# A fused attention and expert layer on one core: feature inputs turned by VectorE, low parts on GpSimd, gate logits behind the last expert, new orders and banks

## What is computed

```python
x = x + tanh(g_xattn) * performer(layernorm(x), ctx, ctx, random_features)
x = x + tanh(g_ffn) * ffn(layernorm(x), ...)
# performer, 16 heads of 16: q' = exp(q @ F) + eps, k' = exp(k @ F - |k|^2/2 - stab) + eps   (64 features)
#   out[t] = q'[t] . sum_{s<=t} k'[s] v[s] / q'[t] . sum_{s<=t} k'[s]
#   stab is one maximum over the keys of all batches
# ffn: h = rmsnorm(x); q = h Wq; k, v = (h Wdown) Wup; softmax over heads, per token; x += (out Wo)
#   h2 = rmsnorm(x); gate = softmax(h2 Wg + bg); x += sum_e gate_e (h2 We_e)
```

## Time and profile before

| | us |
|---|---|
| median of 3 runs | 1260.78 |
| lowest and highest | 1250.12, 1265.76 |
| span of the profiled execution | 1252.8 |
| TensorE busy | 1193.6 (95%) |
| VectorE busy | 942.0 (75%) |
| ScalarE busy | 728.5 (58%) |
| GpSimd busy | 568.1 (45%) |

### The profile page before, as it was taken

How to read it: one execution, slowest core, us unless ns; L and a number is a source line. 1 busy time by engine, 2 the same in 40 slices (tenths; PEclk the granted TensorE clock), 3 DMA queues, 4 the chain that set the end, 5 groups by cost and what they waited for, 6 DMA issues and landing times.

```text
span 1252.8 us, 55905 instructions
## 1 busy us (share of the span) xinstructions
PE 1193.6 (95%) x25347; PEld 978.2 (78%) x25347; DVE 942.0 (75%) x2206; ACT 728.5 (58%) x1467; POOL 568.1 (45%) x887
## 2 busy tenths in 40 slices
PE   1689899999999999999999999999999999999988
PEld 1467678888888888888888888888788888888876
DVE  7576567787777778777877777777787777777875
ACT  7577545566656556665655665565566656555430
POOL 3455515545444554544445454434545444554320
PEclk9988989999999999999999999999999999999999
DMA  9310000000000000000000000000000000000000
GB/s 304 96 36 20 20 10 29 20 29 28 28 12 28 28 20 28 29 28 11 28 28 20 28 29 28 13 26 29 20 29 28 29 12 28 29 19 11 12 20 17
DMA packets 39005, 40.20 MB, mean 32 GB/s; under 512 B 3440, under 2 KB 38512, under 8 KB 38768
## 3 DMA queue, kind: packets, MB, share of 16 engines
q1 hardware_dynamic: 38384, 36.59, 9.3%
q0 software_dynamic: 384, 0.04, 0.0%
HBM read 28.23 MB, written 8.39 MB: 29 GB/s over the span
## 4 chain that ended last, share of the span: by engine, by line
PE 93%; DVE 2%; DMA 1%; POOL 1%; issue 1%; ACT 1%; SPq 0%; DVEq 0%; POOLq 0%; ACTq 0%
PE ps L1899 14%; PE ps L1901 12%; PE ps L1900 12%; PE ps L1932 10%; PE ps L1947 7%; PE ps L1974 6%; PE ps L1966 6%; PE ps L1940 6%; PE ps L1893 4%; PE ps L1915 4%; PE ps L1957 2%; DMA c_chunk<-in_ctx 1%; PE ps L1982 1%; PE ps L2238 1%; PE ps L2336 1%
## 5 line engine op out<-in xcount | busy, mean ns | idle before, releaser
L1200 DVE SCALAR_TENSOR_TENSOR z<-ps,gate,z 128x256 f32<-128x256 f32 x512 | 245.4, 479 | 80.2 <-PE ps L1901 68.4
L1899 PE MATMUL ps<-we_hi,h_hi 128*128 128x512 f32 x512 | 215.6, 421 | 2.4 <-DVE z L1200 2.4
L1901 PE MATMUL ps<-we_hi,h_lo 128*128 128x512 f32 x512 | 203.9, 398 | 0.0
L1900 PE MATMUL ps<-we_lo,h_hi 128*128 128x512 f32 x512 | 203.7, 398 | 0.0
L1932 PE MATMUL ps<-qf,kf 64*128 64x256 f32 x1024 | 133.5, 401 | 5.1 <-POOL kf L474 2.1
L1899 PEld LDWEIGHTS ps<-we_hi,h_hi 128*128 128x128 f32 x512 | 97.4, 190 | 24.6 <-DVE z L1200 3.3
L453 POOL TENSOR_SCALAR z<-y,tanh_f 128x512 f32<-128x512 f32 x32 | 22.1, 692 | 205.5 <-DVE y L1433 205.3
L1932 PEld LDWEIGHTS ps<-qf,kf 64*128 64x128 f32 x1024 | 97.0, 193 | 23.5 <-issue 7.6
L1901 PEld LDWEIGHTS ps<-we_hi,h_lo 128*128 128x128 f32 x512 | 97.1, 190 | 23.0
L1900 PEld LDWEIGHTS ps<-we_lo,h_hi 128*128 128x128 f32 x512 | 97.5, 190 | 16.0
L1947 PE MATMUL ps<-att,v 128*32 128x256 f32 (+1 forms) x2048 | 98.5, 331 | 2.3 <-issue 1.4
(11 more groups left out here) (217 smaller groups left out, 3056.1 us busy)
## 6 DMA issues: line engine op xcount, KB each, us to landing
c_in<-in_ctx SPq DMA_DIRECT2D x32, 256.0 KB, 4.0
x_in<-in_x SPq DMA_DIRECT2D x32, 256.0 KB, 2.8
out<-z SPq DMA_DIRECT2D x32, 256.0 KB, 2.2
c_chunk<-in_ctx SPq DMA_DIRECT2D x14, 512.0 KB, 8.8
stage<-in_L_ffn_We SPq DMA_DIRECT2D x2, 1024.0 KB, 9.3
c_chunk<-in_ctx SPq DMA_DIRECT2D x2, 256.0 KB, 8.2
stage_q<-in_L_ffn_Wq SPq DMA_DIRECT2D x1, 256.0 KB, 8.5
stage_u<-in_L_ffn_Wup SPq DMA_DIRECT2D x2, 128.0 KB, 6.5
```

What stands on the lines that cost most here:

```text
L1200: return dve.scalar_tensor_tensor(out=z[e % 2][:, t, :], in0=ps[:, bank, ex % 2 * D:(ex % 2 + 1) * D], scalar=gate[:, t, ex:ex + 1], in1=z ...
L1899: pe.matmul(out, a_hi(c), b_hi(c), start=(c == 0), stop=False)
L1900: pe.matmul(out, a_hi(c), b_lo(c), start=False, stop=False)
L1901: last = pe.matmul(out, a_lo(c), b_hi(c), start=False, stop=(c == C - 1))
```

## The change

- x, the context and the norms are turned by VectorE in 32x32 blocks (`x_t_`, `c_t_`, `h_tr_`) into x_raw, c_raw and h_raw in SBUF. The ten TensorE transposes of a batch for them are gone. Columns then run over tokens and pairs of heads, and kf and qf are written by `tokens_of` in runs of 32.
- The low parts q_lo and k_lo are subtracted by GpSimd, from SBUF.
- The gate weights stand behind the expert weights (we_hi, we_lo of E*D + E columns). `mm0g` and `mm1g` make expert 7 with the gate logits, 264 columns; `mm03` and `mm13` make expert 6 alone, 256 columns.
- qf and kf have one buffer each.
- The norms are four products of 512 columns for eight of 256.
- All orders, waits and banks are new. SyncE's slot stores first and then loads, five batches apart.

```diff
-            def keys_turned(q):
-                turn(ps[:, BANK["c"], :], c_in[q % 2]).then_inc(*up("c_t", q))
-            def queries_turned(q):
-                turn(ps[:, BANK["x"], :], xn).then_inc(*up("x_t", q))
...
+            def x_t_(b):
+                dve.wait_ge(*at("xn", b))
+                dve.transpose(blocks(x_raw), xn[:, :, :].rearrange("p t (a d) -> p (t a) d", d=32)).then_inc(*up("x_t", b))
+            def c_t_(b):
...
+                dve.wait_ge(*c_load.at(b))
+                dve.transpose(blocks(c_raw), c_in[b % 2][:, :, :].rearrange("p t (a d) -> p (t a) d", d=32)).then_inc(*up("c_t", b))
...
-                dve.tensor_tensor(flat(k_lo), ps[:, BANK["c"], :], flat(k_hi).bitcast(F32), ALU.subtract).then_inc(*up("k_lo", q))
+                pool.wait_ge(*at("k_hi", b))
+                pool.tensor_tensor(k_lo[:, :], c_raw[:, :], k_hi[:, :].bitcast(F32), ALU.subtract).then_inc(*up("k_lo", b))
...
-                expert_products(e, 1, 3, BANK["mm13"]).then_inc(*up("mm13", e))
+                expert_products(b, 1, slice(6 * D, 7 * D), BANK["mm13"]).then_inc(*up("mm13", b))
+            def mm1g_(b):
...
+                expert_products(b, 1, slice(7 * D, E * D + E), BANK["mm1g"]).then_inc(*up("mm1g", b))
```

The new wait list of Y1, of y00's reader, and SyncE's slot:

```diff
             def Y1_(b):
+                if b:
+                    pe.wait_ge(*at("bkv0", b - 1))
+                if b in (0, 1, 2) or b >= 5:
+                    pe.wait_ge(*at("x110", b))
...
+            def av0_(b):
+                pe.wait_ge(*at("m00", b))
+                pe.wait_ge(*at("x011", b))
+                pe.wait_ge(*at("y00", b))
...
             def slot(n):
-                load_x_(n + 2)
-                load_c_(n + 2)
-                write(n - 3)
+                store_(n - 3)
+                load_x_(n + 2)
+                load_c_(n + 2)
```

```diff
-BANK = dict(x000=3, x001=7, x010=5, x011=0, y00=6, y01=5, av0=2, x100=6, x101=5, x110=0, x111=1, y10=3, y11=2,
...
+BANK = dict(stab=0, fk0=2, fk1=4, fk2=1, fk3=6, fq0=6, fq1=3, fq2=1, fq3=2, x000=4, x001=7, x010=1, x011=2,
+            y00=5, y01=3, av0=2, x100=0, x101=1, x110=5, x111=3, y10=7, y11=5, av1=7, nd0=7, nd1=0, ht=3,
+            dn=3, qq=1, kv0=7, kv1=3, s=0, pv=0, otr=5, o=5, h20=1, h21=4, mm0g=4, mm1g=6, mm00=2, mm01=1,
+            mm02=7, mm03=5, mm10=5, mm11=3, mm12=6, mm13=7)
```

More of the change, by code:

```diff
@@ L200, in build @@
[L200 to L205, removed]
@@ L210, in build @@
[L210 to L277, removed]
-        ]
@@ L279, in build @@
[L279 to L281 removed]
+        gammas_in, wq_in, wo_in = transfer("gammas_in", 1, 4), transfer("wq_in"), transfer("wo_in", 1, 2)
+        down_in = transfer("down_in", 1, 6)
+        bqkv_in, wg_in = transfer("bqkv_in", 1, 2), transfer("wg_in", 1, 2)
+        we_in, rf_in = transfer("we_in", 1, 2), transfer("rf_in", 1, 8)
+        signals = [
+            signal("once_pe0", "most_turned stab_all"),
+            signal("pe0", "fq fk X00 av0 X11"),
+            signal("pe1", "Y0 X10 av3 nt_t hn_t dn"),
+            signal("pe2", "X01 Y1"),
+            signal("pe3", "av1 qq kv1"),
+            signal("pe4", "kv0 s3"),
+            signal("pe5", "pv3 o_tr o h2_t0"),
+            signal("pe6", "h2_t1 mm0g mm00 mm10"),
+            signal("pe7", "mm1g mm01 mm12 mm13"),
+            signal("pe8", "mm02"),
+            signal("pe9", "mm11 mm03"),
+            signal("once_dve0", "half zero_v1 v1_one least_ least stabilizer less0 less wup_hi wq_hi wo_lo wg_lo"),
+            signal("keys_dve0", "key_sums"),
+            signal("dve0", "h_lo h_tr"),
+            signal("dve1", "q_st q_mv q_bn x_t"),
+            signal("dve2", "c_t"),
+            signal("dve3", "y01 y10 den_s den_d den o_x g_st g_mv g_bn ht_lo d_lo"),
+            signal("dve4", "y00 y11"),
+            signal("dve5", "bqq q_t k_t smax ssub p_t"),
+            signal("dve6", "bkv1 s_sum s_tok ssum"),
+            signal("dve7", "bkv0"),
+            signal("dve8", "o_tok ot_lo y2 h2_lo0"),
+            signal("dve9", "h2_lo1 ga gmax gm gsum grec gate a1g a0g a00_ a00 a01_ a01 a02_ a02"),
+            signal("dve10", "a10_ a10 a11_ a11 a12_ a12 a13"),
+            signal("dve11", "a03"),
+            signal("keys_act0", "square"),
+            signal("act0", "h_hi"),
+            signal("act1", "xn q_hi eq3 ek3 x000"),
+            signal("act2", "h_t"),
+            signal("act3", "k_hi eq2 eq1 ek1"),
+            signal("act4", "eq0 ek2 x010 x110 x111"),
+            signal("act5", "ek0 x001 x100 x101 nt1"),
+            signal("act6", "x011 nt0 hn ht_hi d_hi"),
+            signal("act7", "q_bd p_bd"),
+            signal("act8", "s_exp ot_hi sq"),
+            signal("act9", "h2n h2_hi1 gexp"),
+            signal("act10", "h2_hi0"),
+            signal("once_pool0", "zero_id ident f_scale f_hi f_lo tri"),
+            signal("pool0", "rstd q_r q_lo k_lo pk0 m00"),
+            signal("pool1", "v1 m01 m10 m11"),
+            signal("pool2", "x1 r_f g_r"),
+            signal("pool3", "o_n z_y z0 ms_e r2"),
+        ]
```

3462 lines of the change are left out of this document (1719 added, 1743 removed).

## The result

The changed kernel takes 1310.03 us (median of 4 runs, 1301.58 to 1313.42) beside 1259.8 for the kernel before on the same chips: a ratio of 1.0402, 95% interval [1.0339, 1.0464]. It is 4% slower where 3% faster was forecast. The profiled execution spans 1311.6 us.

What follows compares the result with a forecast made beforehand. TensorE's own instruction stream was taken as the bound: 1252.8 us, less 55.7 for 34.65 us batches, plus 14.9 for the Y1 stall, gives 1212.0, and 8 on top makes 1220 us. Range 1200 to 1248 us.

Steps and rivals of the forecast that it cites:

- nothing but TensorE's own instruction stream sets the time: Steady state of the kernel before: TensorE busy 398.61 of 400 us, one batch every 36.39 us.
- the walk of the new slot: Waits of the new order followed with the rows' durations from X01's end: Y1 0.55 us late, the next margins thin.
- The thin margins break: Rival: four waits with 0.3 us to spare cost 0.5 to 1.2 us a batch, 1233 to 1252 us; chance 0.22.
- the load behind the store: Rival: x's load queued behind the store delays av0; landing 6.0 us behind it loses the gain, 6.6 gives 1279; chance 0.06.
- The other side, 0.03: Whole kernel: chance 0.03 of coming out slower, above 1286 us, priced by store and load running one after another.
- What leaves and comes to TensorE: TensorE per batch: 1.88 us leaves and 0.14 comes, 36.39 to 34.65 us, with ends 34.55 and 34.95.
- the 1.88 us: TensorE per batch: gate products 0.88, transposes of norms 0.20, c_in 0.44 and xn 0.36 leave.
- the sum: Whole kernel: 55.7 us less from shorter batches, 14.9 more from the Y1 stall, 1252.8 to 1212.0, plus 8 gives 1220.
- one more seam of any kind: TensorE: blocks of one kind go from 23 to 24 a batch, costing 0.10 us, or 0.3 if a seam costs twice.
- Y1 behind x110: Second keys: Y1 waits for ScalarE's copy x110 (bank 5), ready at 5.60 against 5.15; 0.55 us a batch with weight load.
- The start and the end: First and last batches and key sums: left as they are, given 8 us either way.
- The 8 us that the prediction estimated by that rule, at fq: VectorE and GpSimd excluding each other: fq, waiting for a1g behind gate, up to 0.3 us late a batch, 8 us more.

Runs made afterwards that it cites:

- few10: Changed kernel, each head block issuing 8 matmuls of 160 columns for 32 of 16, only some tokens computed: 1216.92 us, ratio 0.9678.
- spread2: Changed kernel, all its work, 32x32 head blocks spread apart on TensorE, some VectorE and ScalarE steps reordered: 1278.6 us, ratio 1.0161.
- before_few10: Kernel before, each head block issuing 8 matmuls of 160 columns, only some tokens computed: 1242.65 us, ratio 0.988.
- loads_first: Changed kernel with SyncE's slot ordered as in the kernel before, x and c loads ahead of the store: 1319.47 us, ratio 1.0495.
- before_clustered: Kernel before with head blocks s0 to s3 in one run ahead of mm01 and mm02, same work: 1374.59 us, ratio 1.0912.

## Why the prediction was wrong, point by point

**The step that failed** is the first: "nothing but TensorE's own instruction stream sets the time" was read as a sum of block durations. The stream has a second limit, the instructions themselves, and the walk of the new slot had no term for it. The order was walked for who waits for whom, and nobody asked how many instructions stand in a row. The price: 38.6 - 35.5 = 3.1 us in a batch, 96 us between the changed kernel's span and few10's (1311.6 - 1215.2), 11 of them ahead of the first h2_t0. By the windows from 600 to 1000 us, 10.4 batches: idle (400 - 380.36) / 10.4 = 1.9 a batch against some 0.3 in few10, and busy 36.7 against 35.3. So about 1.6 us are idles, and 1.4 us longer matmuls. Of these 0.8 are the clock (0.98 over 400 us, so 8 us in 10.4 batches); the other 0.6 I can't place.

The profile before had the sign, in the first row of its waits between 150 and 1250 us (L1966 is head_scores):

```profile
PE ps L1966 <- issue: 4.2, 3, 3.1
```

These waits are few, up to 3.1 us long, and have no releaser; the earlier trace rows has 8704 matmuls in 400 us, thus 17400 instructions, 68 pieces, 5.9 us each on average, and the two head blocks of the earlier trace rows in one row (x128, 256 instructions with the loads) eat one in 1.2 us. One such pair the fetch could cover; that nothing was left to cover a second one close by was to be asked. The Trainium skill, page "Runtime: NRT & Kernel Launch", section "Instruction fetch mechanics", states that an engine's instructions come in blocks of 16 KiB, 256 of them, fetched ahead while the engine runs, and that a boundary's cost is mostly hidden. The size is as the trace has it (198 packets for 3.24 MB). That it is hidden holds for most steady batches of the kernel before, and not here.

**The rivals.** Each was a wait for an engine or a transfer. "The thin margins break" and "the load behind the store" are small: fq, hn_t, dn and X00 never waited for more than a few tenths in the steady part, and av0's waits for y00, behind x's statistics, come to 8.2 us in all. From 400 to 1200 us x lands 3.9 us behind the store's issue (median; 3.2 to 5.0), just as the walk had it, and never at the 6.0 that would have used up the gain. VectorE did wait for it at the statistics (8.8 us between 600 and 1000, 9 times), and a part of that can have reached av0. The other side, 0.03, was priced by the wrong mechanism.

**What leaves and comes to TensorE.** Without the supply's part a batch goes from 36.45 to 35.5, not from 36.39 to 35.2. TensorE's busy time is 35.31 (35.45 in the changed kernel's best batch) where 34.65 was costed and 34.95 was its upper end: the 1.88 us left, but what remains takes longer. Most of it stands in the head blocks. In the earlier trace rows 128 of their matmuls take 603.18 to 604.38, 1.20; in the changed kernel 64 take 0.66:

```profile
605.32 0.74 PE L1888 MATMUL ps<-v_t,p_t 32*32 32x16 f32 x64
605.98 1.14 PE L1846 MATMUL ps<-qf,kf 64*128 64x256 f32 x8
```

Four such pairs of blocks make 4.8 us before; the eight single ones make 5.5 in the batch from 601.24 (one of them takes 0.9). So these seams alone cost some 0.7, where the sum had 0.10 for one more seam of any kind. Counting kinds of blocks was right, one price for all was not: spread2 has 0.5 us more of busy time where blocks were taken apart.

**Y1 behind x110.** The mechanism is there:

```profile
614.54 1.16 PE L1854 MATMUL ps<-qf,kf 64*128 64x128 f32 x16 [0.23 <-ACT att L736]
```

It was put at 0.55 and is 0.23 here, 0.13 on average in few10 (3.7 us in the run), since TensorE came to it later: X01 ends at 608.80 and TensorE is ready for Y1 at 614.31, 5.5 us for the 5.15 walked. The two errors took each other away in part: 0.3 us a batch over in sum. That few10's 1216.92 stands beside the forecast 1220 is luck: the sum had 41 us of gain, measured are 26, and the same edit took 15 from the kernel before.

**The start and the end** were given 8 us either way. Without the supply's part that was enough: of the 26.3 us between the spans of few10 and before_few10, 23.7 lie in the 28 batches from the first h2_t0 on. The first h2_t0 comes 11 us later (125.5 for 114.5), and the end is 14 us shorter.

**What was right.** VectorE has 28.8 us a batch and GpSimd 19.8, for 28.9 and 19.9; the exponentials take 0.60, x_t 0.71. var_f lost its collision:

```profile
631.19 0.17 DVE L1159 TENSOR_SCALAR var_f<-mvg 128x2 f32<-128x2 f32 x1
...
616.34 0.61 DVE L1345 TENSOR_TENSOR h2e<-hk,h2e 128x32 f32<-128x32 f32 x1
```

0.17 for the 1.20 of the earlier trace rows. The second row, earlier in the batch, is h_lo, 32 elements wide (0.76 on average from 600 to 1000 us), which starts while q_lo runs on GpSimd (615.62 to 616.91) and ends with it at 0.61; so the rule of the Trainium skill's page "SBUF — State Buffer", section "SBUF: two separate sides", that such operations shut each other out, fits this row as well. The 8 us that the prediction estimated by that rule, at fq, didn't come: no wait of fq for VectorE stands among TensorE's waits from 600 to 1000 us.

**What is left open.** Why the granted clock fell more often in loads_first than in the changed kernel; whether the share of half clock could be had back by itself; how many instructions, at what distance, the fetch just covers.

## What to carry to other kernels

Beside each engine's busy time, count its instructions; matmuls and weight loads each count. Here a piece of 256 came in 3.3 us at best, and the fetch was at most one piece ahead. One stretch of 256 in 1.2 us was mostly covered; 640 in 6.6 us, and 512 in 2.4 us (before_clustered), were not, and which batch paid depended on where the stretch fell in the pieces. Such blocks are to be kept apart by long ones, and an order that packs them together for the sake of another engine must earn more than that. Read "issue" as a cause of its own: a wait that ends in the middle of a block, with no releaser, and periods that vary in a cycle, are its marks.

## What was not expected of the hardware

- Instructions of TensorE came in packets of 16 KB, the next one as a rule about 1 us after the piece before it began, never two less than 3.28 us apart (3.2 in the kernel before), and a stalled TensorE went on 2.2 to 2.9 us after the packet's start; 5 or 24 GB/s of other traffic made no difference.
- Moving two expert blocks past two head blocks cost 117 us of 1257, with no change in work (before_clustered); about half of it came by the lower clock.
- An idle of 0.7 to 1.7 us was at times followed by 3 us or more at a granted clock of 0.50, which added 0.8 us a batch to the 1.6 of the idles themselves.
